# Decoder layer: attention scores from 48 stacked rows, and more tile slots for the experts

## The reference

```
x = x + fuse(mamba_forward(ln(x)), mamba_backward(ln(x)))      # state size 32, inner size 512
# cross-attention, 16 heads of 16
q = ln(x) @ Wq.T; k = ctx @ Wk.T; v = ctx @ Wv.T
attn = softmax(q_h . k_h / 4) over 361 keys, for each batch and head
x = x + (attn @ v_h, heads joined) @ Wo.T + bo
# experts: the top 2 of 8 (256 -> 1024 -> 256, silu), and a shared one
y = ln(x)
x = x + sum over the 2 picked e of cw[e] * (silu(y @ W1[e] + b1[e]) @ W2[e] + b2[e]) + 0.1 * shared(y)
```

## Time and profile before

| what | before |
|---|---|
| median of 3 runs | 1074.85 us (1071.8 to 1075.17) |
| the profiled execution | 1072.01 us |
| its span | 1070.3 us |
| TensorE busy | 971.9 us, 91% |
| VectorE busy | 888.1 us, 83% |
| ScalarE busy | 818.5 us, 76% |
| GpSimd busy | 681.6 us, 64% |
| granted TensorE clock, mean | 0.955 |

### The profile page before, as it was taken

The page is one execution under the profiler, slowest core; times in us unless marked ns, Lnnn a source line. Parts: engine busy times, 40 slices in busy tenths (PEclk is TensorE's granted clock), DMA queues, the critical chain, the costliest instruction groups (busy, mean ns, idle before and its releaser), DMA issues.

```text
span 1070.3 us, 17480 instructions
## 1 busy us (share of the span) xinstructions
PE 971.9 (91%) x6032; PEld 696.0 (65%) x6032; DVE 888.1 (83%) x1027; ACT 818.5 (76%) x1802; POOL 681.6 (64%) x417
## 2 busy tenths in 40 slices
PE   5994898998999989899998999798989989999995
PEld 3543555655656656566565567577767689899995
DVE  7798999999999999999999997666677754665663
ACT  4999999998999999999899851565556655676763
POOL 2001999999999999999999984751120025254442
PEclk9996899999999999999999999899899979999998
DMA  6001344444444434444444432310000009799973
GB/s 196 9 8 45 102 113 111 109 114 110 113 110 110 112 110 113 111 111 112 109 112 111 113 73 68 126 29 15 15 2 2 2 2 334 243 368 324 331 214 57
DMA packets 86775, 122.22 MB, mean 114 GB/s; under 512 B 11127, under 2 KB 79984, under 8 KB 86672
## 3 DMA queue, kind: packets, MB, share of 16 engines
q1 hardware_dynamic: 82848, 115.78, 37.4%
q0 software_dynamic: 3840, 5.34, 2.5%
HBM read 115.92 MB, written 5.99 MB: 114 GB/s over the span
## 4 chain that ended last, share of the span: by engine, by line
PE 40%; DVE 29%; issue 12%; DMA 10%; ACT 7%; POOL 1%; DVEq 0%; POOLq 0%; ACTq 0%
DVE states L1905 16%; PE ps L1337 14%; DMA sums<-y_tile,token_of 9%; PE ps L1229 6%; DVE states L1883 5%; PE ps L1317 4%; PE ps L1212 3%; PE ps L1470 3%; PE ps L1482 2%; DVE neg_max L2021 2%; ACT probs L1099 2%; PE ps L1498 1%; PE ps L1325 1%; PE ps L1222 1%; PE ps L1517 1%
## 5 line engine op out<-in xcount | busy, mean ns | idle before, releaser
L743 POOL TENSOR_TENSOR states<-states,c_row 128x800 f32<-128x800 f32 x255 | 473.2, 1912 | 89.4 <-DVE states L1905 89.1
L1337 PE MATMUL ps<-states,ident 128*128 128x400 f32 x1024 | 381.0, 508 | 11.4 <-DVE u L1913 11.4
L1337 PEld LDWEIGHTS ps<-states,ident 128*128 128x128 f32 x1024 | 186.9, 192 | 116.7 <-DVE u L1913 12.7
L1905 DVE TENSOR_TENSOR_SCAN states<-sb_decay,ps 128x800 f32<-128x800 f32 x128 | 231.9, 1812 | 4.7 <-ACT sb_decay L1013 3.9
L1905 DVE TENSOR_TENSOR_SCAN states<-ps,states 128x800 f32<-128x800 f32 x128 | 230.2, 1798 | 1.1 <-ACT ps L1013 1.1
L1005 ACT ACTIVATE xT<-xn_tok,xT 100x256 f32<-100x256 f32 x512 | 216.4, 493 | 0.6 <-PE ps L1317 0.2
L1013 ACT ACTIVATE ps<-dt,neg_a 128x396 f32<-128x396 f32 x256 | 141.2, 583 | 45.1 <-DVE states L1905 44.2
L1317 PEld LDWEIGHTS ps<-ident,xT 100*128 100x128 f32 x1024 | 101.1, 145 | 81.2 <-issue 62.8
L1013 ACT ACTIVATE sb_decay<-dt,neg_a 128x396 f32<-128x396 f32 x256 | 144.4, 611 | 1.0 <-DVE states L1905 0.9
L1317 PE MATMUL ps<-ident,xT 100*128 100x100 f32 x1024 | 114.8, 257 | 29.4 <-DVE states L1905 17.6
L1099 ACT ACTIVATE probs<-ps,neg_max 100x361 f32<-100x361 f32 x128 | 70.9, 560 | 65.0 <-DVE neg_max L2021 64.4
(11 more groups left out here) (273 smaller groups left out, 1643.6 us busy)
## 6 DMA issues: line engine op xcount, KB each, us to landing
c_row<-rows SPq DMA_DIRECT2D x256, 200.0 KB, 3.1
w_tile<-in_w SPq DMA_DIRECT2D x40, 1024.0 KB
b_row<-rows SPq DMA_DIRECT2D x32, 200.0 KB, 3.1
ctx<-in_ctxT SPq DMA_DIRECT2D x8, 361.0 KB, 3.9
win<-in_winT SPq DMA_DIRECT2D x2, 1024.0 KB, 10.9
shared_raw<-in_w SPq DMA_DIRECT2D x2, 1024.0 KB, 6.6
wout<-in_woutT SPq DMA_DIRECT2D x2, 512.0 KB, 6.5
token_rows<-rows_src SPq DMA_DIRECT2D x1, 828.1 KB
```

What stands on the lines that cost most here:

```text
L743: nc.gpsimd.tensor_tensor(st, st, c_row[i % C_SLOTS][:].unsqueeze(1).broadcast_to([P, CP, TQ]), ALU.mult).then_inc(product_ready, 1)
L1337: mm = nc.tensor.matmul(ps[:, j, 0:TQ], ident[:], states[i % RING][:, j * TQ:(j + 1) * TQ], start=(n == 0), stop=(n == N - 1), skip_group_ ...
L1905: nc.vector.tensor_tensor_scan(st, rates, inflows, 0.0, ALU.mult, ALU.add).then_inc(scan_done, 1)
```

## The change

**Scores.** The three parts of a head's keys stand under one another as 48 rows (3 x 16), and the queries' high, low and high parts opposite to them (keys high, high, low; queries high, low, high), so that one matmul sums all three products. The two heads of a group are at rows 0 to 47 and 64 to 111. To put the parts in place each batch's keys are stored to a table in DRAM (`k_rows`, four stores of the high part and two of the low by SyncE, each 8 heads x 16 x 362), and GpSimd's queue reads them back in two DMAs of 48 x 8 x 362 into `k_stack`. Queries go the same way, in halves of 400 tokens. The masks and the second copy of the queries are gone, and `kT_part` has one buffer instead of two.

**Order.** Keys are made two batches ahead, at group 7 and at group 0 of the batch behind it; values at groups 3 and 4. Keys and values of batches 0 and 1 are made ahead of the loop, in banks of the job list (`bank_jobs`). Heads are taken in another order, so `wo_sb` is loaded in 8 pieces and `wv` split in 4 operations. The third transpose of a head covers 105 columns in place of 128. The loops on SyncE and GpSimd are written out, and the blank rows are stored behind the contexts.

**Tiles.** W_SLOTS 4 to 6, X_SLOTS 5 to 6, `y_tile` 2 to 4. The added slots lie over tiles that are no longer used then (`rows_src`, `xn3T`, the shared expert's `hidden`), so load 4 waits for `hid_ready` and three others, and fetch 5 for `hidden_used`.

```diff
-W_SLOTS, X_SLOTS = 4, 5
+HIDDEN_SLOTS = 4
+W_SLOTS, X_SLOTS, Y_SLOTS = 6, 6, 4
+FIRST_W, FIRST_X, FIRST_Y = 4, 5, 2
...
-MASS_AT, PROJECT_AT, KEYS_AT, VALUES_AT = 1, 2, (3, 4), (5, 6)
+HEAD_CONSTS = 2
...
+STACKED = 3 * HD
...
+KEYS_HIGH, KEYS_LOW, QUERIES_HIGH, QUERIES_LOW = (0, 1), 2, (0, 2), 1
...
-        q_part = [[sb(f"q_{n}{i}", [P, KD, T], F32R, scope=attn) for n in "hl"] for i in range(PAR)]
-        kT_part = [[sb(f"kT_{n}{r}", [P, KD, SE], F32R, scope=attn) for n in "hl"] for r in range(2)]
+        q_part = [sb(f"q_{n}", [P, KD, T], F32R, scope=attn) for n in "hl"]
+        kT_part = [sb(f"kT_{n}", [P, KD, SE], F32R, scope=attn) for n in "hl"]
+        q_stack = sb("q_stack", [P, STACKS, T], F32R, scope=attn)
+        k_stack = [sb(f"k_stack{r}", [P, STACKS, SE], F32R, scope=attn) for r in range(2)]
+        q_rows = nc.dram_tensor("q_rows", [H, STACKED, T], F32, kind="Internal").ap()
+        k_rows = [nc.dram_tensor(f"k_rows{r}", [H, STACKED, SE], F32, kind="Internal").ap() for r in range(2)]
         probsT = [[sb(f"probsT{r}{j}", [P, KT * L], scope=attn) for j in range(QUADS)] for r in range(2)]
         ctx_sb = [sb(f"ctx{r}", [P, KD, S], scope=attn) for r in range(2)]
...
+        def block_rows(i):
+            return slice(i * BLOCK, i * BLOCK + STACKED)
+        def keys_at(b, g):
+            if g == GROUPS - 1 and b + 2 < B:
+                return b + 2, 0
+            if g == 0 and 1 <= b < B - 1:
+                return b + 1, 1
+            return None
...
-            for w_dram, w_sbuf in ((wqT, wq_sb), (wkT, wk_sb), (wvT, wv_sb), (woT, wo_sb)):
+            for w_dram, w_sbuf in ((wkT, wk_sb), (wvT, wv_sb), (wqT, wq_sb)):
...
+                    sp.dma_start(wo_sb[at:at + HD], by_head[par, j]).then_inc(wo_in, 16)
...
+            def store_part(rows, parts, at, signal):
+                for m in range(KD):
+                    heads = rows[m * HT:(m + 1) * HT, at * HD:(at + 1) * HD, :]
+                    sp.dma_start(heads, parts[:, m, :].bitcast(F32)).then_inc(signal, 16)
+            def store_keys(b):
+                r = b % 2
+                if b >= 2:
+                    sp.wait_ge(k_stacked[r], 16 * 2 * (b // 2))
+                sp.wait_ge(k_high, KD * (b + 1))
+                for at in KEYS_HIGH:
+                    store_part(k_rows[r], kT_part[0], at, k_stored[0][r])
+                keys_copied(sp, b, KD - 1)
+                store_part(k_rows[r], kT_part[1], KEYS_LOW, k_stored[1][r])
+            def store_queries(q):
+                rows, high, low = (t[:, :, chunk(q)] for t in (q_rows, *q_part))
+                sp.wait_ge(q_high, KD * (q + 1))
+                for at in QUERIES_HIGH:
+                    store_part(rows, high, at, q_stored[q])
+                job_copied(sp, ("qT", KD - 1, q))
+                store_part(rows, low, QUERIES_LOW, q_stored[q])
+            def load_context(b):
+                sp.wait_ge(ctx_split, 2 * (b - 1))
+                sp.dma_start(ctx_sb[b % 2][:], ctxT[b].rearrange("(k p) s -> p k s", p=P)).then_inc(ctx_in[b % 2], 16)
+            load_context(2)
+            store_keys(0)
+            store_queries(0)
+            store_keys(1)
+            load_context(3)
+            store_queries(1)
...
+                elif k == FIRST_W:
+                    sp.wait_ge(tokens_ready, 1)
+                    sp.wait_ge(cwT_done, 1)
+                    sp.wait_ge(token_rows_stored, 16)
+                    sp.wait_ge(hid_ready, UNITS)
...
+            def load_stack(to, rows, signal):
+                for i in range(2):
+                    nc.gpsimd.dma_start(to[block_rows(i)], rows[i::2].rearrange("t r s -> r t s")).then_inc(signal, 16)
+            def stack_keys(b):
+                r = b % 2
+                if b >= 2:
+                    pool.wait_ge(scores_ready, GROUPS * (b - 1))
+                pool.wait_ge(k_stored[0][r], 16 * 4 * (b // 2 + 1))
+                pool.wait_ge(k_stored[1][r], 16 * 2 * (b // 2 + 1))
+                load_stack(k_stack[r], k_rows[r], k_stacked[r])
+            def stack_queries(q):
+                pool.wait_ge(q_stored[q], 16 * 6)
+                load_stack(q_stack[:, :, chunk(q)], q_rows[:, :, chunk(q)], q_stacked[q])
...
+            stack_keys(0)
+            stack_queries(0)
...
+            stack_keys(1)
+            split_context(2)
+            stack_queries(1)
...
+                if k == FIRST_X:
+                    pool.wait_ge(hidden_used, UNITS)
...
-                for i in range(PAR):
-                    ins = nc.scalar.activation(q_part[i][0][:, m, chunk(q)], bank(("qT", m, q))[:, 0:TQ],
-                                               ACT.Identity, scale=par_mask[:, i:i + 1])
-                ins.then_inc(q_high, 1)
-            act.wait_ge(mask_ready, 1)
+                nc.scalar.activation(q_part[0][:, m, chunk(q)], bank(("qT", m, q))[:, 0:TQ], ACT.Copy,
+                                     scale=HD ** -0.5).then_inc(q_high, 1)
+            def high_keys(b, m):
+                keys_done(act, b, m)
+                if b:
+                    act.wait_ge(k_stored[0][(b - 1) % 2], 16 * 4 * ((b + 1) // 2))
+                src = bank(("kT", b, m))[:, 0:SE] if b < FIRST_BATCHES else ps[:, KEY_BANK, 0:SE]
+                nc.scalar.activation(kT_part[0][:, m, :], src, ACT.Copy).then_inc(k_high, 1)
...
             def scores(b, r, g):
-                m = 2 * g // HT
-                if g % (GROUPS // KD) == 0:
-                    pe.wait_ge(k_copied, 2 * b + (m + 1))
-                if not isinstance(b, int) or GROUPS * b + g >= 2:
+                if g == 0:
+                    pe.wait_ge(k_stacked[r], 16 * 2 * (b // 2 + 1))
+                    if b % BQ == 0:
+                        pe.wait_ge(q_stacked[b // BQ], 16 * 2)
+                if GROUPS * b + g >= 2:
                     pe.wait_ge(probs_ready, 2 * GROUPS * b + (2 * g - 2))
-                for n, (hi, lo) in enumerate(((0, 0), (0, 1), (1, 0))):
-                    for i in range(2):
-                        _, j, par = head_at(2 * g + i)
-                        rows = slice(j * QUAD, (j + 1) * QUAD)
-                        mm = nc.tensor.matmul(ps[0:L, g % 2 * 2 + i, 0:SE],
-                                              q_part[par][hi][rows, m, b * L:(b + 1) * L],
-                                              kT_part[r][lo][rows, m, :], start=(n == 0), stop=(n == 2))
+                for i in range(2):
+                    mm = nc.tensor.matmul(ps[0:L, g % 2 * 2 + i, 0:SE],
+                                          q_stack[block_rows(i), g, b * L:(b + 1) * L],
+                                          k_stack[r][block_rows(i), g, :], start=True, stop=True)
                 mm.then_inc(scores_ready, 1)
             def turn_probs(b, g):
                 pe.wait_ge(probs_ready, 2 * GROUPS * b + (2 * g + 2))
...
+                        cols = key_tile(kt)
+                        mm = nc.tensor.transpose(ps[0:cols.stop - cols.start, 4 + j, kt * L:(kt + 1) * L],
+                                                 probs[g % 2][:, j, cols], ident[0:L, 0:L])
...
+                    if keys_at(b, g):
+                        keys(*keys_at(b, g))
+                    if values_at(b, g):
+                        values(*values_at(b, g))
...
+                if k >= Y_SLOTS:
+                    dve.wait_ge(tile_added, 16 * (k - Y_SLOTS + 1))
+                nc.vector.tensor_scalar(y_tile[k % Y_SLOTS][:], ps[:, 6 + k % 2, 0:D], weight[k % 2][:], None, ALU.mult
                                         ).then_inc(tile_weighed, 1)
```

More of the change, by code:

```diff
@@ L190, in bank_jobs @@
         jobs.append((("fuse", h), "v"))
+    for m in range(KD):
+        jobs.append((("kT", 0, m), "v"))
     for q in range(Q):
         for k in range(KD):
-            jobs.append((("xn2T", k, q), "v" if q else "a"))
+            jobs.append((("xn2T", k, q), "a"))
+        if q == 0:
+            jobs.append((("v", 0, 1), "a"))
+        else:
+            for m in range(KD):
+                jobs.append((("kT", 1, m), "v"))
         for m in range(KD):
             jobs.append((("qT", m, q), "v"))
+        for b, part in (((0, 0),), ((1, 1), (1, 0)))[q]:
+            jobs.append((("v", b, part), "v" if b else "a"))
     for q in range(Q):
@@ L475, in decoder_layer @@
         y_gated = sem("y_gated")
-        probs_zeroed = sem("probs_zeroed")
-        mask_ready = sem("mask_ready")
+        q_stored = [sem(f"q_stored{q}") for q in range(Q)]
+        k_stored = [[sem(f"k_stored_{n}{r}") for r in range(2)] for n in ("high", "low")]
+        q_stacked = [sem(f"q_stacked{q}") for q in range(Q)]
+        k_stacked = [sem(f"k_stacked{r}") for r in range(2)]
         v_zeroed = sem("v_zeroed")
@@ L647, in _ @@
             sp.dma_start(b2_sb[:], b2).then_inc(moew_in, 16)
+            for b in range(FIRST_BATCHES, B):
+                store_keys(b)
+                if b + 2 < B:
+                    load_context(b + 2)
             sp.wait_ge(route_consts, ROUTE_CONSTS)
```

(19 more changed lines are left out.)

312 lines of the change are left out of this document (180 added, 132 removed).

## The result

The change is slower by 6%: 1141.84 us (median of 4, 1135.85 to 1147.05) against 1075.01 before, a ratio of 1.060 with a 95% interval of 1.056 to 1.064. The profiled execution took 1135.85 us (before: 1072.01), its span is 1134.1. I forecast 1062, with a range up to 1092. It went the way of the rival with the long trip, past its price of 1087 and, as it says for what comes behind the waits, beyond 1092.

What follows compares the result with a forecast made beforehand. PE was taken to bound attention and tile stage, with DMA engines also full in the latter. -13.2 + 6.0 - 4.6 - 1.3 + 7.5 - 7 = -12.6 from 1072.0 gives 1059.4, with 2.8 for the median 1062; range 1051 to 1092.

Steps and rivals of the forecast that it cites:

- the rival with the long trip: Attention batches: keys' way through DRAM takes up to 14.6 us, PE idles at group 6, about 1087 us; chance 0.30.
- the trip: Attention batches: keys go to DRAM and back in 11 us, 10.0 hidden, so 1.0 a batch shows, +6.0 for six.
- the start: Before batch 0: first scores wait for keys and queries to pass through DRAM, +7.5 us, bounds +4 and +12.
- the tile stage: After attention: more tiles hide waits and weight loads end sooner, so the last scatter comes 7 us earlier; bounds 0 and -9.
- trip + 9.2: Batch period if the way through DRAM is long: 5.0 us ahead of it, 4.2 from `scores(b,0)` to the end.
- PE's saving: Attention batches: fewer score matmuls and smaller transposes free 3.0 us of PE, 2.2 taken as gain, -13.2 for six.
- Batch 0: First attention batch: saves its 2.2 us and 2.4 for batch 1's products made ahead of the loop, -4.6 in all.
- the two waits for `x_tile`: Tile stage: PE's two waits cost 7.8 us with what follows; a sixth row tile was to hide both.
- The score pair: Each attention group: one score pair of 0.25 us remains, two pairs of three going at 0.17 each.
- the rival with a product worth two: Attention scores: a 48-row pair takes as long as two, +11 us over eight batches, 1073, no change; chance 0.08.

Runs made afterwards that it cites:

- e1: The change, but keys and queries copied straight from tile to tile by SyncE, without DRAM table or read-back: 1079.0 us, ratio 0.999 to the kernel before.
- e5: e1 with each part of a head copied to every third row of the 48 instead of 16 rows in a run: 1072.3 us, ratio 0.998.
- e6: e5 with batch 0's queries copied ahead of everything else: 1064.5 us, ratio 0.988.
- e16: e6 run once more, the same kernel: 1067.8 us, ratio 0.989.
- e8: The change without stores and read-backs of keys in batches 2 to 7, whose scores use stacked keys of batches 0 and 1: 1094.1 us, ratio 1.016.
- e4: The kernel before with only the tile stage's part: six weight slots, six row tiles, four output tiles: 1073.3 us, ratio 0.995.
- e12: e4 with four weight slots as before, so only the row and output tiles added: 1071.9 us, ratio 0.994.

## Why the prediction was wrong

- **The failing step is the trip**: "I take 11", between ends of 9.0 and 14.6. It is 19.4 us. Three of its four terms were too small: issues 4.0 and not 2.0 (0.6 to 1.0 us each, and nearly all six behind the low copy), landing of the stores 5.3 and not 1.8, read-back 8.9 and not some 6; only GpSimd's issues were 1.3 as taken. Both ends came from rows of loads over 128 partitions or of 100 KB. None of those showed a transfer of this shape, and an end taken from the nearest row was no bound. The rule of the Trainium skill on 8 of 16 engines ("DMA: Bandwidth & Descriptors", the section named above) pointed the right way for the stores, and I had it as a rival only.
- **The rival's mechanism was right, its sum partly by luck.** 7 x (19.4 - 11) is 58.8; with the start 18.5 worse than forecast and the tile stage 3.8, -12.6 becomes +68.5, against +63.8 measured. But PE waited for `k_stack` six times and not seven (55.0 us), as the keys of batches 0 and 1 are stored early; with six it is +60.1. A period is 29.6 us and not trip + 9.2 = 28.6, with the half clock behind each wait. The mechanism and its place (PE at `scores(b,0)` in group 6) were right; its size was taken for the less likely.
- **The start** was forecast at +7.5 with bounds of 4 and 12, and is +26.0. First scores: 688 forecast, 708.67 measured. Keys' and queries' transfers were priced as if each had the DMA engines to itself, while 2.3 MB are stored in a row and read back again; from the low copy to the first scores it was 29.1 us, 18.8 in e1, 14.1 in e5 and 7.5 to 8.5 in e6 and e16, where fewer bytes stand ahead.
- **PE's saving** was forecast at 2.2 us a batch, and it is 2.1 at full clock (e8, e5); PE's busy time fell from 19.4 to 16.6, 2.8 us where 3.0 were worked out. Over the four batches the saving was 2.2 in e5 (22.3 to 20.1), 0.8 in e6, 0.3 in e8. That PE would be on the half clock in more batches, even without a trip, was not in the sum.
- **Batch 0** gave 6.6 us from its first transposes to the next batch's spreading (27.3 to 20.7), where 4.6 was forecast.
- **The tile stage**: -7 forecast, -3.2 in the trace, and 5 by e4 and e12. The loads did end more than two tiles sooner, but the scatters beside them came 8.3 us apart and not 7.76, and one of the two waits for `x_tile` stayed (2.7 us).
- **The score pair** was to take 0.25 us and takes 0.33, from its start to that of the next operation; before, the three took 0.67. That is the 0.34 of the sum, so the rival with a product worth two fell; how much of the two heads overlaps wasn't measured.

```profile
717.49 0.41 PE L1637 MATMUL ps<-k_stack,q_stack 48*100 48x362 f32 x2
717.82 0.73 PE L1668 MATMUL ps<-probsT,v 128*32 128x100 f32 x24
```

## What to carry over

Price a DMA by a row of the same shape, not of the same size: which partitions it writes decided here between 5.0 and 8.8 us for the same rows, and a bound from another shape is none. When a matmul is taken from an engine that waits for others, look at the granted clock of the batches afterwards, and not at the saved time alone; six products that nobody needs, put into a wait that is there anyway, gave back more than they cost, and twelve did not. Whether they would help the kernel before, which has a batch on the half clock too, wasn't run. The round trip through DRAM for a mere change of partitions could be a straight copy here.
